# Transposing the normalised x on VectorE and through a DRAM scratch, not on TensorE

## The reference: what is computed

```
def mixer(u):                      # u [16, 512, 128]
    Bu = u @ B_w.T                 # 64 states
    h = real(ifft(fft(eig**t) * fft(Bu)))[:512]    # per state: a causal convolution over time
    return h @ C_w.T + D * u
def experts(x):                    # 8 experts, hidden width 512, every token through every expert
    cw = softmax(x @ w_router) * softmax(x @ w_gating / 0.1); cw = cw / sum(cw)
    return sum_e cw[e] * ((silu(x @ w_gate[e]) * (x @ w_up[e])) @ w_down[e])
x = x + layernorm(mixer(layernorm(x)))
x = x + layernorm(experts(layernorm(x)))
```

## Time and profile before

| | |
|---|---|
| median of 3 runs | 1169.93 us (1169.41 to 1170.9) |
| the profiled execution | 1171.27 us, of which the span from first to last instruction 1169.4 us |
| mean granted TensorE clock | 0.992 |
| busy share of the span | PE 98%, DVE 81%, ACT 58%, POOL 55% |
| DMA | 57.60 MB, 82,696 packets |

### The profile page before, as it was taken

One profiled execution on the slowest core, in us unless ns is written; L12 is line 12 of the kernel. 1 busy time (PEld: TensorE's weight loads), 2 busy tenths in 40 slices (PEclk: granted clock), 3 DMA queues, 4 the chain that ended last, 5 costly groups with the idle time before them and its releaser, 6 DMA issues.

```text
span 1169.4 us, 16900 instructions
## 1 busy us (share of the span) xinstructions
PE 1144.2 (98%) x5156; PEld 940.8 (80%) x5156; DVE 946.0 (81%) x2045; ACT 673.4 (58%) x1293; POOL 640.3 (55%) x496
## 2 busy tenths in 40 slices
PE   7899999999999999999999999999999999999996
PEld 6678888888888888888888888888888888888885
DVE  8688788888878888787888878878887888878765
ACT  2366565565656556565655656556565655656563
POOL 4467465555646455464555646555454645556453
PEclk8899999999999999999999999999999999999999
DMA  3230210202121020211102121020211102021110
GB/s 122 63 109 28 64 45 16 68 28 73 37 55 37 19 82 28 64 46 37 46 28 73 36 64 46 22 62 28 73 38 48 44 19 82 28 68 33 47 51 12
DMA packets 82696, 57.60 MB, mean 49 GB/s; under 512 B 35344, under 2 KB 64176, under 8 KB 82608
## 3 DMA queue, kind: packets, MB, share of 16 engines
q1 hardware_dynamic: 82608, 56.54, 16.4%
HBM read 48.13 MB, written 8.39 MB: 48 GB/s over the span
## 4 chain that ended last, share of the span: by engine, by line
PE 95%; DVE 3%; issue 1%; POOL 0%; ACT 0%; DMA 0%; POOLq 0%; SPq 0%; ACTq 0%; DVEq 0%
PE g L263 10%; PE u L263 10%; PE u L265 10%; PE u L264 10%; PE g L264 10%; PE g L265 10%; PE y L263 10%; PE y L265 10%; PE y L264 10%; PE n_ps L270 2%; PE m_ps L263 1%; PE m_ps L265 1%; PE m_ps L264 1%; PE m_ps L335 1%; PE y L286 1%; PE m_ps L336 1%
## 5 line engine op out<-in xcount | busy, mean ns | idle before, releaser
L1001 POOL TENSOR_TENSOR hid_lo<-hid,hid_hi 128x512 fp32r<-128x512 f32 x255 | 341.1, 1338 | 410.8 <-ACT hid_hi L493 410.7
L487 ACT ACTIVATE gate<-g 128x512 f32<-128x512 f32 x512 | 306.1, 598 | 340.1 <-PE g L265 339.4
L743 DVE TENSOR_TENSOR hid<-gate,u 128x512 f32<-128x512 f32 x512 | 348.2, 683 | 161.2 <-ACT gate L487 128.6
L493 ACT ACTIVATE hid_hi<-hid 128x512 fp32r<-128x512 f32 x512 | 321.6, 628 | 57.2 <-DVE hid L743 56.5
L263 PE MATMUL g<-xe_hi,w_hi 128*128 128x512 f32 x512 | 206.8, 404 | 0.0
L749 DVE TENSOR_TENSOR hid_lo<-hid,hid_hi 128x512 fp32r<-128x512 f32 x257 | 202.3, 787 | 1.8
L263 PE MATMUL u<-xe_hi,w_hi 128*128 128x512 f32 x512 | 200.2, 391 | 2.3 <-DVE hid L743 2.3
L263 PE MATMUL y<-hid_hi,w_hi 128*128 128x512 f32 x512 | 199.8, 390 | 0.2 <-ACT hid_hi L493 0.2
L265 PE MATMUL g<-xe_hi,w_lo 128*128 128x512 f32 x512 | 199.8, 390 | 0.0
L264 PE MATMUL g<-xe_lo,w_hi 128*128 128x512 f32 x512 | 199.8, 390 | 0.0
L265 PE MATMUL u<-xe_hi,w_lo 128*128 128x512 f32 x512 | 199.7, 390 | 0.0
(11 more groups left out here) (151 smaller groups left out, 1171.1 us busy)
## 6 DMA issues: line engine op xcount, KB each, us to landing
cw_b<-cw_scratch SPq DMA_DIRECT2D x128, 256.0 KB, 3.3
x_sb<-x_in SPq DMA_DIRECT2D x16, 256.0 KB, 3.0
x_out<-o_sb SPq DMA_DIRECT2D x16, 256.0 KB, 2.2
out_scratch<-acc_t SPq DMA_DIRECT2D x60, 64.0 KB, 2.3
ffn<-out_scratch SPq DMA_DIRECT2D x15, 256.0 KB, 2.7
stage<-wgate_in SPq DMA_DIRECT2D x8, 256.0 KB, 2.7
stage<-wup_in SPq DMA_DIRECT2D x8, 256.0 KB, 3.1
stage<-wdown_in SPq DMA_DIRECT2D x8, 256.0 KB, 4.1
```

The lines of the kernel that those rows point to most:

```text
L487: nc.scalar.activation(gate[:, k % 2, :], g_ps[k % 2][:], ACT.Silu).then_inc(gate_ready, 1)
L493: nc.scalar.activation(hid_hi[:, k % RING, :], hid[:, k % RING, :], ACT.Copy).then_inc(hi_ready, 1)
L743: nc.vector.tensor_tensor(hid[:, k % RING, :], gate[:, k % 2, :], u_ps[k % 2][:], ALU.mult).then_inc(hid_ready, 1)
L1001: nc.gpsimd.tensor_tensor(hid_lo[:, k % RING, :], hid[:, k % RING, :], hid_hi[:, k % RING, :].bitcast(f32), ALU.subtract).then_inc(lo_pool, 1)
```

## The change

For chunks 1 to 15 the four transposes of `xn` on TensorE go away. DVE transposes `xn` in 32x32 blocks into a new tile `xn_b` after unit 4 (`mix_turn_x`, now in DVE's list). SP waits for it, issues four transfers of 64 KB that lay the blocks out in the new DRAM scratch `xn_scratch` (`turn_xn`), waits for them, and loads the scratch back into the new tile `xn_t` (`load_xn`). In SP's order both stand after the spread for expert 2 (in chunk 0 after the spread for expert 0), ahead of the spread for expert 3 and of `turn_blocks`. ACT and DVE read `xn_t` in place of `n_ps`, and ACT's unit 8 now waits for that load. `mix_lo_x` moves from unit 7 to unit 8 of DVE's list. In the prologue `keep_warm_split` and TensorE's wait for `act_hi` ahead of it are taken out. The wait for `cw_t_ready` that stood before the transposes of x moves to `mix_turn_y`. Chunk 0's own x is transposed as before.

```diff
--- before.py
+++ after.py
@@ -41,11 +41,11 @@
 PIECES = WCOLS // F
 
 
-TENSOR_AT = {"turn_cw": 4, "turn_x": 5, "bu": 9, "c": 15, "turn_y": 16, "turn_xe": 26,
+TENSOR_AT = {"turn_cw": 4, "bu": 9, "c": 15, "turn_y": 16, "turn_xe": 26,
              "logits": 27}
 SCALAR_AT = {"cw_t": 3, "hi_x": 8, "du": 8, "hi_w": 13, "fin_a": 19, "fin_b": 20, "z_a": 18, "z_b": 18,
              "hi_xe": 26, "silus": 28}
-VECTOR_AT = {"weights": 1, "stats_x": 1, "var_x": 2, "norm_x": 3, "lo_x": 7, "enter": 8, "scan": 9,
+VECTOR_AT = {"weights": 1, "stats_x": 1, "var_x": 2, "norm_x": 3, "turn_x": 4, "lo_x": 8, "enter": 8, "scan": 9,
              "fin_turn": 6, "fin_stats": 14, "fin_var": 14, "fin_shift": 15, "leave": 12, "lo_w": 13, "y": 15, "stats_y": 16, "var_y": 16,
              "shift": 18, "stats_x1": 22, "var_x1": 22, "norm_x1": 24, "lo_xe": 26, "softmax": 27, "exps": 30,
              "products": 31}
@@ -57,7 +57,7 @@
 SPLIT_BEFORE = (8, 10)
 SMALL = 32
 PROJ = P + D + 2 * E
-FIN_STORED = 16 * (D // SMALL)
+FIN_STORED = XN_STORED = 16 * (D // SMALL)
 X1S = 3
 
 POOL_LO = (1, 3)
@@ -85,6 +85,7 @@
     wdown_v = wdown_in.rearrange("e (b p) h -> e p b h", p=P)
 
     out_dram = nc.dram_tensor("out_scratch", [SEQ, D], f32, kind="Internal").ap()
+    xn_dram = nc.dram_tensor("xn_scratch", [D, SEQ], f32, kind="Internal").ap()
     cw_dram = nc.dram_tensor("cw_scratch", [2, E * NT, P], f32, kind="Internal").ap()
 
     with ExitStack() as ctx:
@@ -120,6 +121,7 @@
         x1 = sb("x1", [P, X1S, NT, D])
         o_sb = sb("o_sb", [P, NT, D])
         acc_t, ffn = sb("acc_t", [P, SEQ]), sb("ffn", [P, NT, D])
+        xn_b, xn_t = sb("xn_b", [P, SEQ]), sb("xn_t", [D, SEQ])
         trig = sb("trig", [P, SEQ])
 
         proj_hi, proj_lo = sb("proj_hi", [P, P + D], f32r), sb("proj_lo", [P, P + D], f32r)
@@ -170,6 +172,7 @@
         down_done, part_ready, part_added = sem("down_done"), sem("part_ready"), sem("part_added")
         fin_link, fin_turned, fin_var, fin_rstd = sem("fin_link"), sem("fin_turned"), sem("fin_var"), sem("fin_rstd")
         fin_stored, fin_loaded = sem("fin_stored"), sem("fin_loaded")
+        xn_blocked, xn_stored, xn_loaded = sem("xn_blocked"), sem("xn_stored"), sem("xn_loaded")
         fin_shift, fin_z, fin_ready = sem("fin_shift"), sem("fin_z"), sem("fin_ready")
 
         MIX_LINKS, SOFT_LINKS, FIN_LINKS, ADDS = 11, 8, 3, E - 1
@@ -208,6 +211,21 @@
                 row = row.rearrange("(a t) -> a t", a=1).broadcast_to([P, SEQ])
                 sp.dma_start(cw_b[:, e % 4, :], row).then_inc(cw_spread[e % 4], 16)
 
+            def turn_xn(c):
+                sp.wait_ge(xn_blocked, c)
+                if c > 1:
+                    sp.wait_ge(xn_loaded, 16 * (c - 1))
+                blocks = xn_dram.rearrange("(a r) (j b c) -> b r j a c", r=SMALL, j=NT, c=SMALL)
+                for b in range(P // SMALL):
+                    sp.dma_start(blocks[b], xn_b[b * SMALL:(b + 1) * SMALL, :].rearrange("r (j a c) -> r j a c", j=NT, c=SMALL)
+                                 ).then_inc(xn_stored, 16)
+
+            def load_xn(c):
+                sp.wait_ge(xn_stored, XN_STORED * c)
+                if c > 1:
+                    sp.wait_ge(act_lo_ready, 2 * c - 1)
+                sp.dma_start(xn_t[:], xn_dram).then_inc(xn_loaded, 16)
+
             def turn_blocks(c):
                 sp.wait_ge(fin_turned, c + 1)
                 if c > 0:
@@ -242,6 +260,9 @@
                 store_cw(c, par)
                 for e in range(E):
                     spread_cw(c, par, e, first)
+                    if e == (0 if first else 2) and not last:
+                        turn_xn(c + 1)
+                        load_xn(c + 1)
                     if e == 3 and not first:
                         turn_blocks(c - 1)
                         load_blocks(c - 1)
@@ -287,24 +308,6 @@
                                             ident[:].unsqueeze(1).broadcast_to([P, 2, P]), start=True, stop=True)
                 return last
 
-            def keep_warm_split():
-
-
-                w = proj_hi[:, 0:P]
-                for i in range(8):
-                    nc.tensor.matmul(y_ps[1][:, 0:SEQ - P], w, act_hi[:, 0:SEQ - P], start=True, stop=True)
-                for i in range(8):
-                    nc.tensor.matmul(y_ps[1][:].rearrange("p (a t) -> p a t", a=2), w,
-                                     act_hi[:, 0:HALF].unsqueeze(1).broadcast_to([P, 2, HALF]), start=True, stop=True)
-                for i in range(8):
-                    nc.tensor.matmul(y_ps[1][:].rearrange("p (t a) -> p t a", a=2), w,
-                                     act_hi[:, 0:HALF].unsqueeze(2).broadcast_to([P, HALF, 2]), start=True, stop=True)
-
-            def mix_turn_x(c):
-                pe.wait_ge(xn_ready, 2 * c + 1)
-                pe.wait_ge(cw_t_ready, c)
-                turn(n_ps, lambda j: xn[:, j, :]).then_inc(xn_turned, 1)
-
             def mix_bu(c, prologue=False):
                 if prologue:
                     pe.wait_ge(trig_link, 1)
@@ -321,6 +324,7 @@
 
             def mix_turn_y(c, first):
                 pe.wait_ge(y_ready, c + 1)
+                pe.wait_ge(cw_t_ready, c)
                 turn(n_ps, lambda j: y_sb[:, j * P:(j + 1) * P]).then_inc(y_turned, 1)
 
             def mix_turn_xe(c):
@@ -380,8 +384,6 @@
             keep_warm(WARM[0])
             turn_tiles(0).then_inc(xn_turned, 1)
             keep_warm(WARM[1])
-            pe.wait_ge(act_hi_ready, 1)
-            keep_warm_split()
             pe.wait_ge(proj_split, 2)
             mix_bu(0, prologue=True)
             keep_warm(WARM[2])
@@ -406,8 +408,6 @@
                     if k == (4 if first else TENSOR_AT["turn_cw"]):
                         mix_turn_cw(c)
                     if not last:
-                        if k == TENSOR_AT["turn_x"]:
-                            mix_turn_x(c + 1)
                         if k == TENSOR_AT["bu"]:
                             mix_bu(c + 1)
                         if k == TENSOR_AT["c"]:
@@ -434,11 +434,16 @@
                 nc.scalar.activation(w_hi[:, e, cols], stage[:, e % 2, cols], ACT.Copy).then_inc(w_hi_done, 1)
 
             def mix_hi_x(c):
-                act.wait_ge(xn_turned, c + 1)
-                nc.scalar.activation(act_hi[:], n_ps[:], ACT.Copy).then_inc(act_hi_ready, 1)
+                if c == 0:
+                    act.wait_ge(xn_turned, 1)
+                else:
+                    act.wait_ge(xn_loaded, 16 * c)
+                src = n_ps if c == 0 else xn_t
+                nc.scalar.activation(act_hi[:], src[:], ACT.Copy).then_inc(act_hi_ready, 1)
 
             def mix_du(c):
-                nc.scalar.activation(y_sb[:], n_ps[:], ACT.Copy, scale=d_col[:]).then_inc(du_ready, 1)
+                src = n_ps if c == 0 else xn_t
+                nc.scalar.activation(y_sb[:], src[:], ACT.Copy, scale=d_col[:]).then_inc(du_ready, 1)
 
             def mix_hi_w(c):
                 act.wait_ge(w_ready, c + 1)
@@ -612,9 +617,16 @@
                 dve.wait_ge(rstd_ready, 3 * c + 1)
                 normalise(xn, lambda j: x_sb[:, j, :]).then_inc(xn_ready, 1)
 
+            def mix_turn_x(c):
+                dve.wait_ge(xn_ready, 2 * c + 1)
+                if c > 1:
+                    dve.wait_ge(xn_stored, XN_STORED * (c - 1))
+                nc.vector.transpose(xn_b[:], xn[:].rearrange("p j d -> p (j d)")).then_inc(xn_blocked, 1)
+
             def mix_lo_x(c):
                 dve.wait_ge(du_ready, c + 1)
-                nc.vector.tensor_tensor(act_lo[:], n_ps[:], act_hi[:].bitcast(f32), ALU.subtract).then_inc(act_lo_ready, 1)
+                src = n_ps if c == 0 else xn_t
+                nc.vector.tensor_tensor(act_lo[:], src[:], act_hi[:].bitcast(f32), ALU.subtract).then_inc(act_lo_ready, 1)
 
             def mix_enter(c):
                 dve.wait_ge(bu_ready, c + 1)
@@ -906,6 +918,8 @@
                             mix_var(c + 1, 1)
                         if k == VECTOR_AT["norm_x"]:
                             mix_norm_x(c + 1)
+                        if k == VECTOR_AT["turn_x"]:
+                            mix_turn_x(c + 1)
                         if k == VECTOR_AT["lo_x"]:
                             mix_lo_x(c + 1)
                         if k == VECTOR_AT["enter"]:
```

## The result

The changed kernel takes 1223.59 us (median; four executions of 1218.72, 1222.11, 1225.08 and 1229.73), the kernel before 1169.72 beside it: ratio 1.0458, 95% interval 1.044 to 1.0477. It is 4.6% slower. The forecast was 1210 us, with 1188 to 1222 for its mechanism, in a range of 1176 to 1240, and 0.86 for slower. The profiled execution took 1218.72 us with a span of 1216.9, so 47.5 us more span than before.

What follows compares the result with a forecast made beforehand. TensorE, busy 98% of the span, was taken as the bound. 1171.27 + 30.2 (round trip) + 9.8 (late landings) + 0.6 (chunk 0) = 1211.9 us profiled, 1.34 less for the median: about 1210, range 1176 to 1240.

Steps and rivals of the forecast that it cites:

- Bound and removal: TensorE's list: each removed group of four transposes gains 0.49 us; with the waits for xn, at most 9.5 us.
- DVE's transpose, the moved expert-sum trip, the traffic: DVE's 0.71 us block transpose fits idle time; turn_blocks and load_blocks start later without delaying their reader: no cost.
- The round trip in a quiet chunk: From block stores through load to mix_bu: TensorE starts 2.16 us later per chunk, 30.2 us over 14 chunks.
- the split of the 4.99 us: First block store to load: 3.55 us for the transfers themselves plus 1.44 for three spreads queued in front.
- Late landings: Irregularly late cw_t and block stores, formerly hidden, now on the path: 0.7 us a chunk, 9.8 us in all.
- Chunk 0: First chunk's trip, with one spread queued before the stores: 0.6 us lost, bounds -2.0 and +3.
- The clock: TensorE's clock falling after its idle gaps in the chunks: left out of the likeliest sum, kept as a rival.
- The rival with a chance of 0.20: TensorE's clock falls after idling in chunks, 3.4 us a stretch: 1234 us in half the chunks, 1258 in all.
- The rule on 128x128 transposes: Trainium skill's advice to transpose on TensorE if a PSUM result is acceptable; by it the change is a loss.
- The rival that it is hidden: xn_t lands by 486.11 in almost every chunk, so 9.5 us are gained: 1160.4 us; chance 0.12.
- The prologue: Before chunk 0's mix_bu, removing the 24 keep-warm matmuls costs no time; bounds 0 and 3 us.
- `mix_lo_x` at 8: Moving it from unit 7 removes a 2.23 us DVE stall, but TensorE did not wait for that: worth nothing.

Runs made afterwards that it cites:

- e1: Kernel before without TensorE's four transposes of x for chunks 1 to 15, nothing in their place: 1164.05 us, ratio 0.9943.
- e2: Kernel before plus the added DVE transposes, four stores and load, read by nobody: 1170.92 us, ratio 1.0003.
- e9: e6 with one table entry changed, mix_lo_x at DVE's unit 7 instead of 8: 1168.08 us, ratio 0.9979 to the kernel before.
- e5: Changed kernel with the block stores and load issued right after the store of cw_t, ahead of all spreads, from chunk 1: 1235.62 us, ratio 1.0574.
- e12: e5 with mix_lo_x back at DVE's unit 7, ahead of the first weighing: 1198.88 us, ratio 1.0259 to the kernel before.
- e3: Kernel before without keep_warm_split and the wait ahead of it, nothing else changed: 1168.55 us, ratio 0.9988.
- e6: e5 with x's statistics, normalisation and block transpose one unit earlier, stores ahead of the store of cw_t, load behind it: 1188.86 us, ratio 1.0167.
- e10: e6 with SP issuing the spread for expert 0 ahead of the load of x, mix_lo_x left at unit 8: 1201.48 us, ratio 1.0272.
- e11: e6 with both edits, mix_lo_x at unit 7 and the spread for expert 0 ahead of the load: 1204.52 us, ratio 1.0284.
- e7: Changed kernel with ten matmuls of 256 columns on the identity ahead of mix_bu of chunks 1 to 15: 1213.22 us, ratio 1.0361.

## Why the prediction was right, step by step

- **Bound and removal.** TensorE is the bound, and what leaves its list is gained: 0.49 us a group forecast, 0.44 measured (e1). 9.5 us was the most that could come; 6.6 came, since the wait for `xn` in chunk 0 only changed its owner.
- **DVE's transpose, the moved expert-sum trip, the traffic: nothing.** Shown by e2, 1.0003. e9, which also reads x from SBUF, shows no loss from that either.
- **The round trip in a quiet chunk: the sum's main term.** Forecast 2.16 us a chunk, measured 2.46. It is made of the steps shown above. That the queue of spreads stands in front of the stores was right, but the split of the 4.99 us was not: with no spread ahead (e5, e12) the stores take 4.2 us to the load, not the 3.55 of `out_scratch`, and the queue adds 0.9, not 1.44. The two errors cancelled.
- **Late landings: too large.** Forecast 9.8 us, measured 4.7, in four chunks. The profiled span grew by 47.5 us: 14 x 2.46 = 34.4, late landings and clock 14.6, chunk 0 +0.1, the start of the first chunk -1.6 (the first store of `cw_t` at 56.96 instead of 58.56).
- **Chunk 0.** 0.6 forecast; with what lies ahead of it -1.5 measured, inside its bounds of -2.0 and +3.
- **The clock: the term that was put at nothing.** The rival with a chance of 0.20 came true in part, on top of the forecast and not in place of it: 9.8 us in the profiled execution, and by mean clock 13 to 22 in the other three (an estimate, with all that was withheld counted as lost work). Without it the measured terms come to 1171.27 + 34.4 + 4.7 - 1.5 - 1.34 = 1207.5 us, so the clock is the whole way to the median, 1223.59, which lies just above the forecast's own 1188 to 1222. That the other terms sum so well is partly luck: late landings were put 5 us too large and chunk 0 2 too large, the round trip 4 too small. The step that failed is leaving the clock out of the likeliest sum, when the visible wait had been worked out at 2.65 us, as long as the stretch of 2.60 ahead of the fall in the earlier trace rows. The rival had the mechanism, but not its price: it took 3.4 us from the earlier trace rows, and here a stretch cost 1.6, since it lasted half as long (505.55 to about 509.0); six in 14 chunks make 10 us, where half the chunks were to make 24. Nor does the length of the wait tell which chunks are hit: the clock fell behind 2.68 us and did not behind 2.94.
- **The rule on 128x128 transposes**: TensorE, where a result in PSUM will do (the Trainium skill, "VectorE: DVE Perf Modes", Rules for kernel authors). As the change stands the measurement agrees, 1.0458; with e9's order the way past TensorE is 0.2% ahead, 0.9979, so it is the schedule that decides.
- **The rival that it is hidden** was short by 2.4 us a chunk, as the rows had said. e9 shows what it takes: an earlier start and `act_lo` out of the weighing's way.
- **The prologue.** 0 to 3 us of loss forecast, a gain of 0.1% measured (e3).
- **`mix_lo_x` at 8: "worth nothing".** True where the spreads come first, as in the changed kernel's quiet chunks. As a statement about the schedule it was too narrow: the move puts `act_lo` behind a second wait, which decides as soon as the spread is the later one (e5 against e12, 37 us; e6 against e9, 21 us).

## What to carry to other kernels

Price a transfer that replaces work of the bounding engine by the time between its first input and its reader's slot, with the order of the queue as it will be, and set that against the slot: here 11.2 us for a slot of 8.8, and 0.44 us of TensorE's work were paid with 2.9 us of its waiting, a net loss of 2.46 a chunk before the clock. Moving the trip forward is not enough: ask which wait becomes the last one, on the reader's engine and on the issuing queue; two instructions swapped on VectorE were worth 37 us, and one spread ahead of the load, with the wait for the small store that this spread reads, cost more than it brought (e10, e11). And where the bounding engine is TensorE, add a slow stretch for some of the waits: here six of fourteen, at 1.6 us each.

## What the runs showed of the hardware that was not expected

- Four stores of equal size and run length did not take equal time. The block stores of `xn_b` are issued in 2.60 us with an empty queue, and the load follows 4.2 us after the first of them (e6, e9, e12); those of `acc_t` took 1.93 to 1.98 and 3.37 to 3.55 in their quiet chunks, in the kernel before. They differ in the layout in DRAM and in the shape of the source view; which of the two counts was not tried.
- A load of 256 KB issued right behind one spread landed after 3.8 us in place of 2.7 (e10 and e11 against e9).
- After a wait of 4.64 us TensorE ran at half clock (505.55 to about 509.0) while it was busy without a gap. The same came after waits of 2.68 and 2.78 us, and did not after one of 2.94 in the same execution, so the length of the wait alone does not decide it. Ten otherwise useless matmuls in the gap made the kernel faster (e7).
